# A third message buffer and a later slot comparison in the edge stage of an attention layer

## What is computed

```python
q_dst = Q[dst]; k_src = K[src]; v_src = V[src]         # 8 heads of 16 features
score = jnp.sum(q_dst * k_src, axis=-1) / np.sqrt(HD)
score = jnp.clip(score, -5.0, 5.0)
attn = jax.nn.softmax(score, axis=0)                   # over all edges, per head
h_out = jnp.zeros_like(Q).at[dst].add(attn[..., None] * v_src)
```

## Time and profile before

| what | value |
|---|---|
| median of three runs | 6164.49 us |
| the profiled execution's own time | 6162.2 us |
| its span | 6160.4 us |
| TensorE matmul busy over the span | 5555.2 us (90%) |
| VectorE, ScalarE, GpSimd busy over the span | 4416.3, 2019.9, 1360.3 us |
| mean granted TensorE clock | 0.967 of full speed |
| edge stage of the attention layer, first to last scatter | 1085.4 to 3257.0 us of the span |

### The profile page before, as it was taken

The page is one execution under the profiler, slowest core; times in us unless marked ns, Lnnn a source line. Parts: engine busy times, 40 slices in busy tenths (PEclk is TensorE's granted clock), DMA queues, the critical chain, the costliest instruction groups (busy, mean ns, idle before and its releaser), DMA issues. The chain is left out here.

```text
span 6160.4 us, 165256 instructions
## 1 busy us (share of the span) xinstructions
PE 5555.2 (90%) x58225; PEld 4851.5 (79%) x58310; DVE 4416.3 (72%) x7547; ACT 2019.9 (33%) x4615; POOL 1360.3 (22%) x1304
## 2 busy tenths in 40 slices
PE   3999988999999999999996879999999998699986
PEld 2888876888888888888885569999999996456655
DVE  7999942777777777777774457777777774388874
ACT  0000033333433434433432322222222221266651
POOL 1444445333333333333332310000000000200000
PEclk9999999999999999999998989999999997899988
DMA  6444412222222222222220123333333330100000
GB/s 122 149 158 149 158 56 79 88 88 85 85 85 85 88 86 82 88 88 81 88 80 18 37 98 117 121 118 118 115 123 117 119 115 34 57 5 0 0 1 22
DMA packets 206210, 523.66 MB, mean 85 GB/s; under 512 B 33555, under 2 KB 85398, under 8 KB 199318
## 3 DMA queue, kind: packets, MB, share of 16 engines
q1 hardware_dynamic: 195936, 518.35, 24.7%
q10 hardware_dynamic: 10179, 4.02, 0.3%
HBM read 485.12 MB, written 37.19 MB: 85 GB/s over the span
## 5 line engine op out<-in xcount | busy, mean ns | idle before, releaser
L1279 PE MATMUL ps<-kv_table,stage 128*128 128x256 bf16 x7644 | 1252.5, 273 | 29.4 <-DVE stage L1135 27.3
L1251 POOL TENSOR_TENSOR message<-message 128x512 f32<-128x512 f32 (+1 forms) x676 | 724.4, 1072 | 1468.9 <-ACT message L1213 1468.9
L1294 PE MATMUL ps<-message,slot_hot 128*128 128x136 f32 x5200 | 779.2, 292 | 121.2 <-POOL message L1251 102.6
L1667 PE MATMUL ps<-a_table,stage 128*128 128x128 bf16 x7644 | 843.7, 219 | 31.3 <-DVE stage L1550 31.3
L1670 PE MATMUL ps<-window,stage 128*128 128x128 bf16 x7800 | 861.3, 219 | 0.0
L1282 PE MATMUL ps<-window,stage 128*128 128x128 bf16 x7800 | 860.6, 219 | 0.0
L1294 PEld LDWEIGHTS ps<-message,slot_hot 128*128 128x128 f32 x5200 | 649.2, 190 | 212.1 <-POOL message L1251 167.8
L1142 DVE TENSOR_TENSOR slot_hot<-iota,slots 128x512 f32<-128x512 f32 (+1 forms) x676 | 452.5, 669 | 452.7 <-PE ps L1294 452.7
L1569 DVE TENSOR_TENSOR slot_hot<-iota,slots 128x512 f32<-128x512 f32 (+1 forms) x676 | 454.1, 672 | 416.5 <-PE ps L1682 401.4
L1620 ACT ACTIVATE edge<-ps 128x512 f32<-128x512 f32 x624 | 373.4, 598 | 1105.9 <-PE ps L1682 1068.8
L1279 PEld LDWEIGHTS ps<-kv_table,stage 128*128 128x128 bf16 x7644 | 669.1, 98 | 71.5 <-issue 27.9
(11 more groups left out here) (335 smaller groups left out, 7606.3 us busy)
## 6 DMA issues: line engine op xcount, KB each, us to landing
stage<-lists SPq DMA_DIRECT2D x312, 768.0 KB, 4.1
edges<-in_edge_attr SPq DMA_DIRECT2D x52, 1984.0 KB, 7.6
stage<-lists SPq DMA_DIRECT2D x104, 896.0 KB, 5.4
window<-qkv_rows SPq DMA_DIRECT2D x52, 288.0 KB, 4.7
qkv_rows<-kv_table SPq DMA_DIRECT2D x26, 384.0 KB, 2.5
window<-ab_rows SPq DMA_DIRECT2D x52, 192.0 KB, 4.3
qkv_rows<-q_parts SPq DMA_DIRECT2D x26, 192.0 KB, 2.0
ab_rows<-a_table SPq DMA_DIRECT2D x26, 192.0 KB, 2.0
```

The lines of the kernel that those rows point to most:

```text
L1251: pool.tensor_tensor(values, values, message[n % 2][:, 0:nt, D:D + HEADS].unsqueeze(3) .broadcast_to([P, nt, HEADS, HEAD]), ALU.mult).then ...
L1279: nc.tensor.matmul(kv_ps[n % 2][:, i, :], from_src, kv_table[:, tile, q, :], start=(q == 0), stop=(q == 2))
L1294: last = nc.tensor.matmul(ps[:, 6 + d, 0:D + HEADS], slot_hot[n % 2][:, i, :], message[n % 2][:, i, :], start=(tile == 0), stop=(tile == S ...
L1667: nc.tensor.matmul(edge_ps[n % 2][:, i, :], from_src, a_table[:, tile, q, :], start=(q == 0), stop=False)
```

## The change

`message` gets a third buffer, laid over the first 544 columns of a new tile `early` that holds the weights and biases named above (that part holds `wqkv_sb` and the head of `bias_qkv`). The buffer is now n % 3 within the pair. A pair has 26 batches, so at its start the rotation breaks: batches 0 and 1 reuse a buffer of two batches before, all others one of three or more before. `scattered1` starts at 3, so `s + 1` now means the scatter of batch s-3 and `s + 2` that of s-2; the other waits on it are shifted to mean the same as before. On VectorE the comparison of slots moves from ahead of `product` to behind the clipping, and still waits for scatter(s-2).

```diff
+        early = sb("early", [P, 13 * D])
+        wqkv_sb = early[:, 0:3 * D]
+        bias_qkv = early[:, 3 * D:6 * D]
+        wo_sb = early[:, 6 * D:7 * D]
...
+            message.append(early[:, 0:4 * (D + HEADS)].rearrange("p (t f) -> p t f", f=D + HEADS))
...
                     def batch(pair, g, n):
-                        dve.wait_ge(scattered1, s + 1)
-                        dve.tensor_tensor(slot_hot[n % 2][:, 0:nt, :], over_chunks(iota1[:, :], nt), ...
                         dve.wait_ge(v_kept1, s + 3)
...
                         dve.tensor_scalar(clipped[n % 2][:, 0:nt, :], score[:, 0:nt, :], CLIP, -CLIP, ALU.min,
                                           ALU.max).then_inc(clipped1, 1)
+                        dve.wait_ge(scattered1, s + 2)
+                        dve.tensor_tensor(slot_hot[n % 2][:, 0:nt, :], over_chunks(iota1[:, :], nt), ...
...
-                        act.wait_ge(scattered1, s + 1)
-                        act.activation(message[n % 2][:, 0:nt, 0:D], kv_ps[n % 2][:, 0:nt, D:2 * D],
+                        act.wait_ge(scattered1, s + 1 if n >= 2 else s + 2)
+                        act.activation(message[n % 3][:, 0:nt, 0:D], kv_ps[n % 2][:, 0:nt, D:2 * D],
...
-                        act.wait_ge(scattered1, pair * NB2 + d * BATCHES + BATCHES + 2)
+                        act.wait_ge(scattered1, pair * NB2 + d * BATCHES + BATCHES + 3)
...
-                    pe.sem_inc(scattered1, 2)
+                    pe.sem_inc(scattered1, 3)
```

More of the change, by code:

```diff
@@ L90, in gnn_program @@
         before = sb("before", [G, G], BF16)
[L91 to L95, removed]
-        we2_sb = sb("we2_sb", [P, D])
+        we2_sb = sb("we2_sb", [P, D])
+        early = sb("early", [P, 13 * D])
+        wqkv_sb = early[:, 0:3 * D]
+        bias_qkv = early[:, 3 * D:6 * D]
+        wo_sb = early[:, 6 * D:7 * D]
+        aw1_sb = early[:, 7 * D:8 * D]
+        aw2_sb = early[:, 8 * D:9 * D]
+        we1_sb = early[:, 9 * D:11 * D]
+        bias_ab = early[:, 11 * D:13 * D]
         wn1_sb = sb("wn1_sb", [P, 2, D])
@@ L103, in gnn_program @@
         be2_sb = sb("be2_sb", [1, D])
-        bias_qkv = sb("bias_qkv", [P, 3 * D])
-        bias_ab = sb("bias_ab", [P, 2 * D])
         sqrt_of = sb("sqrt_of", [1, 2])
@@ L1158, in batch @@
                                           ALU.max).then_inc(clipped1, 1)
+                        dve.wait_ge(scattered1, s + 2)
+                        dve.tensor_tensor(slot_hot[n % 2][:, 0:nt, :], over_chunks(iota1[:, :], nt),
+                                          over_columns(slots[:, ds(g, 1), 0, 4 * b:4 * b + nt]
+                                                       .rearrange("p s t -> p (s t)"), P),
+                                          ALU.is_equal).then_inc(slot_hot1, 1)
                     def add(j, g, d):
@@ L1212, in exp @@
                         act.wait_ge(clipped1, s + 2)
-                        act.activation(message[n % 2][:, 0:nt, D:D + HEADS], clipped[n % 2][:, 0:nt, :],
+                        act.activation(message[n % 3][:, 0:nt, D:D + HEADS], clipped[n % 2][:, 0:nt, :],
                                        ACT.Exp).then_inc(weight1, 1)
                     def group(j, pair, d):
-                        act.wait_ge(scattered1, pair * NB2 + d * BATCHES + BATCHES + 2)
+                        act.wait_ge(scattered1, pair * NB2 + d * BATCHES + BATCHES + 3)
                         act.wait_ge(added1, j + 1)
@@ L1249, in _ @@
                             pool.sem_inc(pool_waited, 1)
-                            values = message[n % 2][:, 0:nt, 0:D].rearrange("p t (h c) -> p t h c", c=HEAD)
-                            pool.tensor_tensor(values, values, message[n % 2][:, 0:nt, D:D + HEADS].unsqueeze(3)
+                            values = message[n % 3][:, 0:nt, 0:D].rearrange("p t (h c) -> p t h c", c=HEAD)
+                            pool.tensor_tensor(values, values, message[n % 3][:, 0:nt, D:D + HEADS].unsqueeze(3)
                                                .broadcast_to([P, nt, HEADS, HEAD]), ALU.mult).then_inc(message1, 1)
@@ L1294, in scatter @@
                             last = nc.tensor.matmul(ps[:, 6 + d, 0:D + HEADS], slot_hot[n % 2][:, i, :],
-                                                    message[n % 2][:, i, :], start=(tile == 0), stop=(tile == SELF))
+                                                    message[n % 3][:, i, :], start=(tile == 0), stop=(tile == SELF))
                         last.then_inc(scattered1, 1)
```

## The result

The changed kernel takes 6003.54 us (median of four runs, 6002.25 to 6005.84) against 6158.90 us for the kernel before (four runs, 6150.59 to 6164.83): ratio 0.9756, 95% interval 0.9743 to 0.9769. It is 155 us faster.

What follows compares the result with a forecast made beforehand. TensorE was nearly the bound, held by a four-engine loop through the V copy. A group takes 27.39 + 11.72 + 0.25 = 39.36 us against 41.67; the 2.31 gain times 52 is 120 us, giving 6044 us, range 6015 to 6095.

Steps and rivals of the forecast that it cites:

- The loop and the third buffer: Edge stage: a loop through the V copy sets 3.23 us; the buffer allows a scatter at 2.80, under TensorE's 3.01.
- The moved comparison: VectorE: behind the clipping, the slot comparison runs 0.03 to 0.72 us after a scatter, free of GpSimd's 1.64 to 2.70.
- The nine intervals: Scatter(0) to scatter(9) of a group: 9 x 3.01 plus 0.3 is 27.39 us against 29.13, a gain of 1.74.
- the pair's charge: Start of a pair: a unit's second comparison meets GpSimd's multiplication, 0.5 us once a pair, 0.25 a group.
- the turn of the group sums: Within scatter(0) to scatter(9) of a group: at most 0.44 us extra, taken as 0.3.
- The four intervals over the short batch: Group's end, around the two-tile batch: 2.80 + 3.01 + 3.01 + 2.90 = 11.72 us against 12.54, a gain of 0.82.
- The collisions of units elsewhere: Units' second comparisons hold GpSimd to about 1.8 us: scatters at 2.9 to 2.95, harmless at batches 3, 6, 9.
- the two at its low end: Whole kernel: 6026 us without collision and pair charge, 6016 with loops also 0.1 us shorter twice a group.
- rival D: Edge stage: TensorE never waits, 37.93 us a group, a gain of 3.74 or 194 us, 5970 us; chance 0.04.
- A: Edge stage: the loop's 0.2 us margin is eaten, period 3.1 us, time 6085 to 6110 us; chance 0.19.
- B: Edge stage: units' second comparisons meet a GpSimd that started first, 0.80 us each, 33 us slower, 6198; chance 0.05.
- C: Edge stage: no change, as VectorE becomes the bound or the clipping stays late for the exponential, 6164 us; chance 0.04.

Runs made afterwards that it cites:

- experiment 2: The slot comparison moved behind the clipping, with two message buffers, against the kernel before: 6154.58 us, ratio 0.9993.
- Experiment 3: The kernel before with GpSimd multiplying only 4 of 8 heads, part of the layer left out: 6000.23 us, ratio 0.9736 against the kernel before.
- Experiment 1: The third buffer alone, slot comparison still ahead of the product, against the kernel before: 6142.18 us, ratio 0.9970.
- experiment 6: The changed kernel with GpSimd multiplying only 4 of 8 heads: 5954.52 us, ratio 0.9668 against the kernel before.
- experiment 7: The changed kernel with ScalarE's exponential ahead of the V copy: 6024.36 us, ratio 0.9783 against the kernel before.
- experiment 8: The changed kernel with the exponential ahead of the V copy and the group's last six tiles as 3 + 3: 6019.79 us, ratio 0.9776 against the kernel before.

## Why the prediction was right and where it was wrong

*The loop and the third buffer: right.* Each start in the period lies within 0.06 us of the forecast, and experiments 2 and 3 show that the loop set the period: it stays at 3.22 us when the comparison alone moves away, and falls to 2.96 when only the multiplication in the loop is made shorter.

*The moved comparison: right about the place, incomplete about its worth.* The prediction found the comparison free of GpSimd at its new place and VectorE not the bound. It did not work out what the buffer would do without the move. Experiment 1 says 139 us less: the comparison's new place is not a detail but the condition of the gain.

*The step that failed.* The prediction says: "Where nothing holds TensorE up it is 3.01 us: 2039.65 to 2042.66 to 2045.67." That term of the sum is too large by 0.05 us: both intervals begin with a scatter whose message came late. The first begins at 2039.65, with a scatter that is listed as held for 1.04 us. The second begins at 2042.66. That scatter is not listed as held, and its matmul is not late either: it starts 0.17 us behind the last matmuls of the gather, as at 2045.50 and 2045.67. But its message was finished only at 2042.61 (2041.55 + 1.06), and its weight load starts together with the matmul, where the next one's starts 0.06 us ahead. In the timeline of the kernel before:

```profile
2041.55 1.06 POOL L1251 TENSOR_TENSOR message<-message 128x512 f32<-128x512 f32 x1 [1.95 <-ACT message L1213]
...
2042.49 0.33 PE L1282 MATMUL ps<-window,stage 128*128 128x128 bf16 x3
2042.66 0.99 PEld L1294 LDWEIGHTS ps<-message,slot_hot 128*128 128x128 f32 x8
2042.66 1.19 PE L1294 MATMUL ps<-message,slot_hot 128*128 128x136 f32 x8
...
2043.69 0.49 PE L1279 MATMUL ps<-kv_table,stage 128*128 128x256 bf16 x3
...
2045.50 0.33 PE L1282 MATMUL ps<-window,stage 128*128 128x128 bf16 x3
2045.61 0.53 PEld L1294 LDWEIGHTS ps<-message,slot_hot 128*128 128x128 f32 x4
2045.67 0.68 PE L1294 MATMUL ps<-message,slot_hot 128*128 128x136 f32 x4
```

Such a scatter of four tiles spends 1.03 us to the next gather (2042.66 to 2043.69); one whose load starts ahead spends 0.98 to 0.99 (2035.89 to 2036.88 after). This holds through the stage. Before, 571 four-tile scatters have the load starting with the matmul and nearly all spend 1.03, and only 52 have it ahead; after, 493 have it ahead, with 0.98 nearly always. The 1.03 that the prediction read was such a late one too (2020.30). So 3.01 was TensorE's period with the price of a late message in it, and 2.96 is its own. Experiment 3 had 2.96 forecast on this ground and measured it.

*The error in numbers.* Trace against trace, the gain was 160 and the forecast 120. A pair takes 77.39 us now and was forecast at 2 x 39.36 = 78.72. All values are medians over the pairs. The nine intervals, with the pair's charge: 27.39 + 26.94 = 54.33 measured, 55.28 forecast; 0.95 x 26 = 25 us. Of this 21 us are the 0.05 in eight of the nine intervals of each group; the turn of the group sums, taken at 0.3, costs 0.23. The four intervals over the short batch: 11.57 + 11.49 = 23.06 measured, 23.44 forecast (the loop gives 2.68 to 2.76, not 2.80, and 3.01 is 2.96 once); 10 us. The group that was read was one of the shorter kind: 41.67, where pairs take 83.47; 3 us. The rest, about 2 us, is not traced to a place.

*The pair's charge: right.* 0.5 was taken; the first group's nine intervals are 27.39 and the second's 26.94, a difference of 0.45, and the collision named is in the trace.

*The collisions of units elsewhere: right.* The multiplications beside them take 1.16 us at most outside the last pair, and no scatter of batches 3, 6 or 9 is late. At batch 0 the forecast charged 0.1 us for such a collision; in the second group of each pair the multiplication there takes its usual 1.06 and starts at 1.65, so the charge was not needed.

*The range.* All its cases rested on the same 3.01, the two at its low end (6026 and 6016) as well. With 2.96 the forecast's own sum is 9 x 2.96 + 0.3 + 2.80 + 2 x 2.96 + 2.90 + 0.25 = 38.81, a gain of 2.86 a group, 149 us. That gives 6015, so this one term is most of the error. A value read from two intervals at one place should have had a bound below it, and rival D's 37.93 was too high for the same reason: experiment 6 reached 37.65 with collisions still in it.

*The rivals.* A did not occur: GpSimd ends 0.26 us ahead of the scatter (2037.54 + 1.06 against 2038.86), and this margin held. The prediction's argument for A, that three of four engines have under 0.9 us of idle per batch, was a misreading: ScalarE and GpSimd are busy 40% and 33% of the time, so each has about 2 us idle in a batch. Only TensorE and VectorE are that full. B's mechanism occurred only where the forecast had put it, at the start of a pair; experiments 7 and 8 made it common. C and D are out: the first by the time, the second because TensorE still waits at batches 10 and 0. The 155 us lie about midway between the forecast's 120 and D's 194, but that is the shorter period, not waits that went.

## What to carry to other kernels

When a wait is taken out of a loop between engines, look for what the waiting engine's new time collides with: here the buffer alone gave 16 us, the move alone 4, and both 155 (in the stage 30, 17 and 163). A lower bound of an engine's period must come from an interval in which its inputs were early; compare the end of the producer with the start of the consumer, and see whether the weight load starts ahead of the matmul, before calling it unheld. Look at the short iteration too: evening out 4 + 2 tiles to 3 + 3 gave another 25 us here.

## What the runs showed of the hardware that was not expected

Which of VectorE and GpSimd starts first decides who pays, and a lead of 0.02 us is enough: 2013.24 against 2013.26 made a comparison of 0.61 us one of 1.46. It recurs at the start of 24 of the 26 pairs. The Trainium skill ("SBUF — State Buffer", SBUF: two separate sides) has this as an exclusive lock of a shared port pair, held for the whole instruction. The traces agree for a two-input comparison (1.55 in place of 0.69 in experiment 1) and for the units' comparisons, and also in that the product, which reads PSUM and one SBUF tensor, runs beside the multiplication at its usual 0.69 us. They differ a little in size. The instruction that came second ends 0.14 to 0.19 us earlier than a wait for the other's whole recorded time would give: the comparison of 2013.26 ends 0.42 us behind the multiplication and takes 0.61 alone, that of 2025.45 in experiment 1 ends 0.55 behind it and takes 0.69 alone.

Time lost this way is not idle time: the held instruction is only longer (1.55 us where 0.69 is usual), so it is found in the spread of durations.

A message that is late by next to nothing costs TensorE about 0.05 us, even where its matmul starts on time (2042.66). The weight load could not start ahead, and the loss is booked behind the matmul, in the distance to the next one (1.03 in place of 0.98).
